# A LoRA-linear kernel on one Trainium2 core: weight differences paused at the first change of phase, and h copied ahead of x at one more change

## What is computed

```python
# x: (32, 128, 2048) f32, one adapter number in 6..15 for each of 32 sequences
result = einsum('bsd,od->bso', x, base_weight) + base_bias   # 2048 x 2048
h      = einsum('bsd,brd->bsr', x, lora_A_w[adapter_ids])    # rank 16
result = result + einsum('bsr,bor->bso', h, lora_B_w[adapter_ids])
return x + result
```

## Time and profile before

| | us |
|---|---|
| median of 3 runs | 1334.47 (1333.99 to 1334.64) |
| the profiled execution's own time | 1329.43 |
| its span | 1327.7 |
| TensorE busy | 1314.6 |
| VectorE busy | 625.5 |
| ScalarE busy | 223.3 |
| GpSimd busy | 203.0 |
| DMA, mean over the span | 233 GB/s |

### The profile page before, as it was taken

One profiled execution on the slowest core, in us unless ns is written; L12 is line 12 of the kernel. 1 busy time (PEld: TensorE's weight loads), 2 busy tenths in 40 slices (PEclk: granted clock), 3 DMA queues, 4 the chain that ended last, 5 costly groups with the idle time before them and its releaser, 6 DMA issues.

```text
span 1327.7 us, 18317 instructions
## 1 busy us (share of the span) xinstructions
PE 1314.6 (99%) x7160; PEld 1207.3 (91%) x7160; DVE 625.5 (47%) x832; ACT 223.3 (17%) x408; POOL 203.0 (15%) x98
## 2 busy tenths in 40 slices
PE   9999999999999999999999999999999999999998
PEld 9999999999997888899999999999888888888887
DVE  4334435645445444556556844345534444533322
ACT  4111212111221000221101211112211111211110
POOL 0000012322210000035454421232000000000000
PEclk9999999999999999999999999999999999999999
DMA  5577777887577777776767845764666788855552
GB/s 201 191 246 243 251 265 259 280 293 246 193 280 262 255 242 232 244 263 243 243 235 274 305 135 167 232 212 158 207 236 240 238 269 297 291 187 192 196 192 108
DMA packets 93658, 308.80 MB, mean 233 GB/s; under 512 B 10498, under 2 KB 19762, under 8 KB 93618
## 3 DMA queue, kind: packets, MB, share of 16 engines
q1 hardware_dynamic: 93618, 308.35, 68.5%
HBM read 211.82 MB, written 97.01 MB: 233 GB/s over the span
## 4 chain that ended last, share of the span: by engine, by line
PE 87%; DMA 5%; SPq 3%; DVE 3%; POOL 1%; issue 1%; ACT 0%; DVEq 0%; ACTq 0%; POOLq 0%
PE acc L944 30%; PE acc L956 28%; PE acc L949 26%; DMA pool<-wT 3%; PE acc L990 2%; SPq L315 1%; DMA pool<-x 1%; SPq L403 1%; POOL pool L878 1%; DMA w_raw<-w_sums 1%; SPq L334 1%; DVE h_cols L768 0%; DMA pool<-xT 0%; SPq L504 0%; SPq L474 0%
## 5 line engine op out<-in xcount | busy, mean ns | idle before, releaser
L956 PE MATMUL acc<-w_lo,x_hi 128*128 128x320 f32 (+2 forms) x2302 | 563.5, 344 | 1.7 <-DVE w_lo L708 1.7
L956 PEld LDWEIGHTS acc<-w_lo,x_hi 128*128 128x128 f32 x2302 | 399.7, 188 | 35.2 <-DVE w_lo L708 2.0
L944 PE MATMUL acc<-w_hi,x_hi 128*128 128x352 f32 x1536 | 334.5, 326 | 0.8 <-ACT w_hi L602 0.8
L944 PE MATMUL acc<-w_hi,x_lo 128*128 128x352 f32 (+1 forms) x1536 | 329.2, 322 | 0.0
L944 PEld LDWEIGHTS acc<-w_hi,x_lo 128*128 128x128 f32 x1536 | 262.3, 189 | 0.0
L944 PEld LDWEIGHTS acc<-w_hi,x_hi 128*128 128x128 f32 x1536 | 258.6, 189 | 1.1 <-DVE w_hi L716 1.0
L949 PE MATMUL acc<-w_hi,x_hi 128*128 128x512 f32 x766 | 241.4, 396 | 0.1
L949 PE MATMUL acc<-w_hi,x_lo 128*128 128x512 f32 x766 | 238.9, 392 | 0.0
L597 ACT ACTIVATE x_hi<-pool 128x1024 fp32r<-128x1024 f32 x110 | 116.2, 1057 | 717.2 <-PE acc L956 361.9
L893 POOL TENSOR_TENSOR pool<-pool,keep 128x1024 f32<-128x1024 f32 x48 | 130.5, 2734 | 409.5 <-DMA pool<-x 409.5
L703 DVE TENSOR_TENSOR x_lo<-pool,x_hi 128x1024 fp32r<-128x1024 f32 x110 | 167.3, 1521 | 49.8 <-ACT x_hi L597 49.8
(11 more groups left out here) (44 smaller groups left out, 410.8 us busy)
## 6 DMA issues: line engine op xcount, KB each, us to landing
pool<-xT SPq DMA_DIRECT2D x142, 512.0 KB, 5.8
pool<-x SPq DMA_DIRECT2D x64, 512.0 KB, 5.6
out<-pool SPq DMA_DIRECT2D x47, 512.0 KB, 2.8
pool<-wT SPq DMA_DIRECT2D x32, 512.0 KB, 7.7
w_sums<-pool SPq DMA_DIRECT2D x32, 512.0 KB, 3.6
w_raw<-w_sums SPq DMA_DIRECT2D x32, 512.0 KB, 6.5
s_sums<-pool SPq DMA_DIRECT2D x32, 512.0 KB, 7.5
pool<-s_sums SPq DMA_DIRECT2D x32, 512.0 KB, 5.3
```

The lines of the kernel that those rows point to most:

```text
L944: mm = nc.tensor.matmul(acc[j][:, o, low:high], xs, w_hi[:, s, base + o * COLS_A + low:base + o * COLS_A + high], start=(k == 0 and part = ...
L956: mm = nc.tensor.matmul(acc[j][:, o, low:low + n], x_hi[:, j, k], w_lo[:, slot(ph, k), first:first + n], start=False, stop=end and (ph not ...
```

## The change

It has three parts. The parts of the weight differences skip places 14, 15 and 16, so that chunks 4 to 7 have places 17 to 28. Each w_raw load of P6 waits on SyncE for the stores of its own chunk (three waits for each of eight loads) in place of the first load's wait for all. And ScalarE copies h ahead of x_high also at P4's last tile and P7's first.

```diff
+PREP_PAUSE, PREP_RESUME = 14, 17
...
 def prep_at(tile):
 
-    n, part = divmod(place(tile) - PREP_FROM, 3)
+    at = place(tile)
+    if PREP_PAUSE <= at < PREP_RESUME:
+        return None, None
+    steps = at - PREP_FROM - (PREP_RESUME - PREP_PAUSE if at >= PREP_RESUME else 0)
+    n, part = divmod(steps, 3)
     return (n, part) if 0 <= n < KC else (None, None)
...
                 else:
+                    if ph == P6:
+
+                        for b, times in zip(PREP_AT, (2, 1, 1)):
+                            sp.wait_ge(pool_out[b], DMA * times * (k + 1))
                     what = w_sums[ph - P6, k]
...
                 if k == 0:
-                    if ph == P6:
-                        for b in PREP_AT:
-                            sp.wait_ge(pool_out[b], DMA * STORES[P2][b])
                     if ph >= 2:
                         sp.wait_ge(summed, TILES * (ph - 1))
...
-                if one.ph == P6 and back.ph == P2:
+                if (back.ph, one.ph) in ((P2, P6), (P4, P7)):
                     h_out(back)
...
-                if place(tile) and back.ph in LORA_PHASES and not (one.ph == P6 and back.ph == P2):
+                if place(tile) and back.ph in LORA_PHASES and not ((back.ph, one.ph) in ((P2, P6), (P4, P7))):
                     h_out(back)
```

## The result

The changed kernel takes 1326.01 us, the median of 4 executions (1325.55 to 1326.35), against 1334.23 of the kernel before (1332.91 to 1334.64): a ratio of 0.9946, 95% interval 0.9928 to 0.9965. Forecast were 1331.8 us and a range from 1328.8 to 1334.4.

What follows compares the result with a forecast made beforehand. TensorE, busy 1314.6 of the span's 1327.7 us, was taken as the bound, so only its idle time could be won. Terms summed to -2.7 us on the profiled 1329.43; adding 5.0 to the median gave 1331.8, range 1328.8 to 1334.4.

Steps and rivals of the forecast that it cites:

- place 16: First tile of P2: TensorE's wait for w_lo of chunk 6 goes with the pause, -1.90 us.
- place 18: Row 2 of P2: TensorE's wait for h_stack goes as the x load is issued earlier, -0.34 us.
- place 79: Last tile of P4: TensorE's wait for h_stack goes when ScalarE copies h ahead of x_high, -1.42 us.
- GpSimd's addition at place 16: First tile of P2: the addition moves to about 200 to 203 and may hold up VectorE's differences, +0.2 us.
- Place 20: Row 4 of P2: the pair of GpSimd operations may newly catch the small h operations, +0.3 us.
- Place 29: Row 13 of P2, after chunk 7's new end: its GpSimd pair may newly catch the h operations, +0.4 us.
- Places 23 and 26: Rows 7 and 10 of P2: the h_cols waits behind GpSimd pairs stay, 2.83 us lost in all as before.
- The waits by chunk: SyncE's three waits for each of eight w_raw loads of P6, all met by then, cost +0.1 us.
- B: Rival, more collisions: all four GpSimd pairs of P2 lose 1.5 us, +0.1 or -0.3 in sum, 1334.2 us; chance 0.16.
- C: Rival: stores and x loads, not wT, delay w_raw; the 1.90 us stay, -0.8 in sum, 1333.7 us; chance 0.07.
- D: Rival, slower: four GpSimd pairs of P2 catch h longest, 2.4 us each, +3.2 in sum, 1337.7 us; chance 0.05.
- A: Rival, collisions go: 23 and 26 lose nothing either as SyncE runs ahead, -6.4 in sum, 1328.1 us; chance 0.20.

Runs made afterwards that it cites:

- e4_waits: Kernel before with only the waits by chunk, without the pause and with ScalarE's order as before: 1330.54 us, ratio 0.9999 to before.
- e8_pause_one: Changed kernel with the pause cut to place 14 alone, so chunk 4 has places 15, 16 and 17: 1334.74 us, ratio 1.0031.
- e1_before: Kernel before, repeated unchanged for a further trace: median 1330.25 us of 12 executions (1327.95 to 1338.32), the profiled one 1338.32.
- e9_after: Changed kernel, repeated unchanged: 1327.23 us (1326.48 to 1329.88) against 1330.35 of before.
- e15_after: Changed kernel, repeated unchanged in the same rounds as before: 1326.58 us (1325.11 to 1327.87) against 1329.79 of before.
- e3_h_first: Kernel before with only h copied ahead of x at P4 to P7: 1331.84 us, ratio 1.0004 to before.
- e14_before: Kernel before, repeated unchanged once more for a further trace: median 1330.67 us of 8 executions (1328.08 to 1336.52).
- e16_best_no_pause: Changed kernel without the pause; GpSimd's last differences (chunks 4 to 7) and additions (P2 rows 0 to 11, P4 rows 0 to 13) wait for h_cols: 1324.94 us.
- e7_stalls: Changed kernel with pieces of x_low repeated on VectorE at five places of P3, so that TensorE waits there: 1343.59 us in one execution.

## Why the prediction was wrong

**Right by the steps, on the execution shown.** The terms, in the order of the sum, against the difference of the two profiled executions: place 16 -1.90, measured -2.0; place 18 -0.34, -0.4; place 79 -1.42, -1.5, though the trace after would have had no such wait anyway. GpSimd's addition at place 16 +0.2, measured 0: it came at 203.87, not 200 to 203. Place 20 +0.3, +0.4. Place 29 +0.4, +0.2. Places 23 and 26 "unchanged": +0.2 and -0.6. The waits by chunk +0.1: no run shows such a price (12.26 us for P6's first tile after 12.29, and e4_waits at 0.9999 of before). The rest of the 3.9 is 0.6 more lost in P4 and 0.7 less in the opening and P1's first tile, which the change does not touch. So the forecast's own terms make 3.3 of the 3.9, where 2.7 were forecast, and of these the 1.5 at place 79 is luck: VectorE's difference was first there, and part 3 had nothing to take away. The mechanism of part 1, w_raw loads behind the wT loads, was confirmed by e8_pause_one, with less cover than forecast: w_lo of chunk 6 was to be there at 201.3 and was near 202. The idle time of a wait was also priced a little low: with 0.16 added in the forecast, the tiles of before lost 0.22 to 0.28 more than the idle time of their wait.

**The step that failed** is the one from the execution to the median: the execution shown "stands 5.0 us under the median of the runs, 1334.47; nothing in the profile says that this part changes, so I take the difference over". Those 5 us are no constant around the span: the changed kernel's profiled execution stood 0.5 us under its median, not 5.0, and that of e1_before 8.1 over its own. In the executions traced later such differences are more of the same waits and 1.7 us of lower clock behind most of the long ones. The slower executions of the first measurement themselves were not traced, so for them this is argued and not shown. The three executions whose range was known lay within 0.7 us of each other and 5 above the profiled one; that was the sign that the trace did not show what they lost. (Among the 143 later executions 1329.43 is an ordinary time.) What the pause removes is worth 2.0 us in the trace shown and 4.6 in e1_before, where place 16 had two waits and a fall.

**The term that was missing** is the clock. I wrote that it stood at its upper level in every slice, which holds for the trace shown, and priced each wait at its own length. In e1_before waits with 2.0 and 2.1 us of idle time cost their tiles 3.8 and 3.9.

**Rivals.** B did not come: places 20 and 29 lose 0.4 and 0.2 us. C is refuted by the w_lo wait that went with the pause and stayed in e8_pause_one. D did not come, but single losses above its 2.4 us exist: three of 3.8 to 4.6 in e1_before, and 3.5 at place 26 in e9_after. A's size came near (1328.1 was given), not its mechanism: 23 and 26 still lose 1.3 us each in the first trace, and 1.5 and 0 in e15_after. "As VectorE ends these differences 10 to 12.5 us into its tile, whatever went before, I expect 23 and 26 unchanged" was too firm: they lose 0.2 to 3.9 in the three traces of before and 0 to 3.5 in the three of the changed kernel.

**How large the gain is.** The first measurement has 8.2 us, from four executions of before at 1332.9 to 1334.6. Of the 143 later ones 33 lie at 1332.9 or above. Later measurements of the same two kernels on single chips have 3.1 and 3.2 us between the medians, near the 2.7 of the sum. If executions were independent, four of four from that part would come in 0.3% of cases (an estimate, 33/143 to the fourth power), so a mere draw is unlikely. Whether that chip favours the slower patterns was not tested and stays open, and with it how much of the first 8.2 us is the change.

## What to carry to other kernels

When the profiled execution lies apart from the others by more than the effect in question, look at a second trace before pricing anything: where waits hang on two engines meeting, one execution is a sample. Price a wait of TensorE near 2 us or more at its length plus the fall of the clock, and cut the long waits first. Two GpSimd operations in a row that read SBUF should not be free to start where VectorE has small operations on the critical chain; one wait on the small operation's semaphore was worth 2 to 3 us (1323.9 against 1326.0 to 1327.2, medians of different measurements) and part of the spread, but look at what the delayed operation meets next.

## What was not expected of the hardware

A fall of the granted clock lasted 3.4 us each time, and in these runs it came behind waits with 2.0 us of idle time and more in all cases but the one of e3_h_first (2.09), and behind some of 1.7 to 1.8 us (e1_before, e4_waits, e8_pause_one, e9_after), not behind others of the same length (before as shown, e14_before, e3_h_first, e16_best_no_pause, e7_stalls). What decides between these was not found. Which of VectorE and GpSimd waits is decided by the start: at place 79 a lead of 0.04 or 0.05 us turned 1.22 and 3.44 us round. The Trainium skill ("SBUF — State Buffer", Who interferes with whom) states that a VectorE instruction with two SBUF inputs contends with a GpSimd instruction that reads SBUF, and that the order of issue decides which of them blocks; the traces agree, with 2.04 us for an operation of 0.17.
